# A twelve-stage transformer kernel: transposing x before it is normalised, centred weights, a second search among the additions, integer slot numbers

## What is computed

```python
# block 0: 7 experts of 512 slots each, the 8th kind passes the token on
x = x + 0.5 * _L0_ffn_ref(_layernorm(x), router_w, router_b, experts_inter, experts_out)
# block 3: 8 linear experts, each token goes to its best two, unweighted
logits = x @ gate_w.T
probs = jax.nn.softmax(logits, axis=-1)
_, topk_idx = jax.lax.top_k(probs, 2)
...
h = _grouped_matmul(moe_in, w_up, seg_ids)
moe_out = _grouped_matmul(h, w_down, seg_ids)
```

## Time and profile before

| | us |
|---|---|
| median of 3 runs (2966.19 to 2968.7) | 2966.94 |
| the profiled execution, its own time | 2966.22 |
| its span in the profile | 2964.5 |
| PE busy, 79% of the span | 2356.5 |
| DVE busy, 68% | 2009.4 |
| ACT busy, 63% | 1861.4 |
| POOL busy, 33% | 974.5 |

### The profile page before, as it was taken

One profiled execution on the slowest core, in us unless ns is written; L12 is line 12 of the kernel. 1 busy time (PEld: TensorE's weight loads), 2 busy tenths in 40 slices (PEclk: granted clock), 3 DMA queues, 4 the chain that ended last, 5 costly groups with the idle time before them and its releaser, 6 DMA issues. The chain is left out here.

```text
span 2964.5 us, 44016 instructions
## 1 busy us (share of the span) xinstructions
PE 2356.5 (79%) x13097; PEld 1220.5 (41%) x13097; DVE 2009.4 (68%) x5780; ACT 1861.4 (63%) x4759; POOL 974.5 (33%) x1296
## 2 busy tenths in 40 slices
PE   4647484738888878499999999997858888888887
PEld 4425453512222246244444444444524444444452
DVE  4616633759899947566666666665568999998854
ACT  2124223327777763377777777776539999999964
POOL 2553275344353332400000000003644444444436
PEclk8778596559999985799999999999769999999979
DMA  6330232023223200000000000000011111111001
GB/s 173 78 53 1 89 69 39 0 42 75 53 49 77 51 8 1 30 1 1 1 1 1 1 1 1 1 1 1 1 34 30 29 30 30 29 30 30 1 1 29
DMA packets 230444, 86.76 MB, mean 29 GB/s; under 512 B 175362, under 2 KB 223298, under 8 KB 230210
## 3 DMA queue, kind: packets, MB, share of 16 engines
q1 hardware_dynamic: 215104, 74.74, 10.8%
q0 software_dynamic: 9856, 7.58, 1.8%
q10 hardware_dynamic: 5250, 1.62, 0.3%
HBM read 26.47 MB, written 15.50 MB: 14 GB/s over the span
## 5 line engine op out<-in xcount | busy, mean ns | idle before, releaser
L2375 ACT ACTIVATE s_pT<-s_ps_t 128x512 f32<-128x512 f32 x1024 | 625.1, 638 | 139.7 <-PE s_ps_t L1975 123.9
L2128 DVE TENSOR_REDUCE s_neg_max<-s_ps_a 128x1 f32<-128x512 f32 x1024 | 666.1, 682 | 63.0 <-PE s_ps_a L1941 53.0
L2366 ACT ACTIVATE s_first<-s_ps_a,s_neg_max 128x512 f32<-128x512 f32 x512 | 390.5, 763 | 25.1 <-DVE s_neg_max L2128 23.4
L2784 ACT ACTIVATE s_e<-s_e,s_neg_max 128x128 f32<-128x128 f32 (+3 forms) x512 | 283.2, 555 | 165.6 <-DVE s_neg_max L2684 163.3
L1987 PE MATMUL s_ps_t<-ident,s_first 128*128 128x128 f32 x2048 | 316.1, 285 | 83.8 <-ACT s_pT L2375 71.3
L2297 POOL TENSOR_SCALAR s_first<-s_first,s_rec 128x512 f32<-128x512 f32 x128 | 232.3, 1815 | 365.6 <-DVE s_rec L2134 359.6
L2684 DVE CUSTOM_DVE_ANT_0 s_e<-s_ps_a,w_alibi 128x128 f32<-128x128 f32 (+3 forms) x512 | 230.7, 487 | 110.9 <-PE s_ps_a L2554 109.9
L1941 PE MATMUL s_ps_a<-s_lanesT 64*128 64x512 bf16 x1024 | 275.2, 401 | 37.3 <-DMA s_lanesT<-n_lanes 20.4
L1987 PEld LDWEIGHTS s_ps_t<-ident,s_first 128*128 128x128 f32 x2048 | 220.8, 141 | 183.5 <-ACT s_pT L2375 141.5
L2002 PE MATMUL s_ps_o<-s_pT,n_v_pad 128*32 128x512 f32 x2048 | 275.9, 612 | 12.2 <-ACT s_oT L2381 12.2
L139 POOL TENSOR_TENSOR s_rstd<-s_ve,minus_half 128x4 f32<-128x4 f32 x24 | 26.4, 1099 | 678.8 <-DVE s_ve L126 678.2
(11 more groups left out here) (382 smaller groups left out, 4079.7 us busy)
## 6 DMA issues: line engine op xcount, KB each, us to landing
s_token_rows<-s_rows SPq DMA_DIRECT2D x4, 1088.0 KB, 5.4
s_x_rows<-x SPq DMA_DIRECT2D x4, 1024.0 KB
x<-s_x_rows SPq DMA_DIRECT2D x8, 512.0 KB, 6.1
s_Wi<-L_ffn_experts_inter SPq DMA_DIRECT2D x2, 1792.0 KB, 8.0
x<-L_attn_x SPq DMA_DIRECT2D x4, 512.0 KB, 7.9
out<-x SPq DMA_DIRECT2D x4, 512.0 KB, 5.3
s_lanesT<-n_lanes SPq DMA_TRANSPOSE x64, 4.1
s_shiftedT<-n_lanes SPq DMA_TRANSPOSE x64, 2.4
```

Source lines behind the costliest of these rows:

```text
L2128: dve.tensor_reduce(neg_max[:, column(n):column(n) + 1], sa[n % NA][:], AX.X, ALU.max, negate=True).then_inc(s.max_ready, 1)
L2366: act.activation(first[:, g % NF, n % PU, :], sa[n % NA][:], ACT.Exp, bias=neg_max[:, n:n + 1], accum_out=sum1[:, n % (NR * PU):n % (NR * ...
L2375: act.activation(pT[:, n % NP, :], st[n % NK][:], ACT.Exp).then_inc(s.probs_ready, 1)
L2784: act.activation(part, part, ACT.Exp, bias=neg_max[:, n:n + 1], scale=-1.0, accum_out=total[:, n:n + 1]).then_inc(s.first_ready, 1)
```

## The change

Five things are changed.

- In the capacity and linear stages TensorE transposes x itself. Subtracting the mean is moved into the weights: `setup` makes a matrix `center` (identity minus 1/128) and multiplies the router's, the gate's and the linear experts' weights by it. The reciprocal deviation is multiplied onto the logits on VectorE, and in the linear stage onto the mask too. The linear stage has no `xn` and no normalisation any more, and two PSUM buffers for the turned batch (one is `y4`). The capacity stage still normalises, for the rows that are gathered, but behind the copies.
- The linear stage's search for the second half of the tokens is cut in four pieces that stand among the additions.
- The numbering of slots uses int32, a shift and a bit mask; `code` is laid out tile by tile.
- ScalarE's exponentials are moved in both stages.
- Semaphores are handed out from a list of free ones, the lowest first, instead of by name. (`lasting` is added, and nothing calls it.)

```diff
@@ -62,18 +62,33 @@
...
-    for n in names.split():
-        if n not in ALL_SEMS.made:
-            ALL_SEMS.made[n] = ALL_SEMS.ctx.enter_context(nc.semaphore(n))
-    return namedtuple("Semaphores", names)(*[ALL_SEMS.made[n] for n in names.split()])
-def clear(nc, s):
-    cleared = range(min(h.num for h in s), max(h.num for h in s) + 1)
...
-    nc.all_engine_barrier(sems_to_clear=cleared)
+    names = names.split()
+    while len(ALL_SEMS.free) < len(names):
+        ALL_SEMS.made += 1
+        ALL_SEMS.free.append(ALL_SEMS.ctx.enter_context(nc.semaphore(f"stage{ALL_SEMS.made}")))
+    taken, ALL_SEMS.free = ALL_SEMS.free[:len(names)], ALL_SEMS.free[len(names):]
+    return namedtuple("Semaphores", names)(*taken)
...
+def clear(nc, s, last=False):
+    numbers = [h.num for h in s]
...
+    nc.all_engine_barrier(sems_to_clear=range(min(numbers), max(numbers) + 1))
+    ALL_SEMS.free = sorted([*s, *ALL_SEMS.free], key=lambda h: h.num)
...
@@ -210,22 +227,36 @@
...
+                pool.tensor_scalar(center[:], G.ident[:], -1.0 / D, None, ALU.add).then_inc(s.made, 1)
...
-                pe.wait_ge(s.made, 1)
+                pe.wait_ge(s.made, 3)
...
+                pe.matmul(psC[:, 0:KINDS], center[:], raw_router[:], start=True, stop=True).then_inc(s.router_psum, 1)
                 multiply_linear(pe)
...
+                pe.matmul(psC[:, 0:KINDS], center[:], raw_gate[:], start=True, stop=True).then_inc(s.gate_psum, 1)
                 turn_adapters(pe)
+                center_linear(pe, center)
...
+                dve.tensor_copy(G.routerT[:], psC[:, 0:KINDS]).then_inc(s.router_copied, 1)
...
+                halve_linear(dve)
...
+                dve.tensor_copy(G.gateT[:], psC[:, 0:KINDS]).then_inc(s.gate_copied, 1)
+                copy_adapters(dve)
                 copy_linear(dve)
-                copy_adapters(dve)
...
@@ -451,12 +491,23 @@
...
-    def copy(dve):
+    def halve(dve):
...
-            dve.tensor_scalar(G.M[:, 4 * i:4 * i + 4, :], ps[i][:], 0.5, None, ALU.mult).then_inc(s.m_copied, 1)
...
+            dve.tensor_scalar(M[:, 4 * i:4 * i + 4, :], ps[i][:], 0.5, None, ALU.mult).then_inc(s.m_halved, 1)
+    def center_rows(pe, center):
+        for i in range(2):
+            pe.wait_ge(s.m_halved, i + 1)
+            pe.matmul(ps[i][:], center[:], M[:, 4 * i:4 * i + 4, :], start=True, stop=True).then_inc(s.centered_psum, 1)
+    def copy(dve):
+        for i in range(2):
+            dve.wait_ge(s.centered_psum, i + 1)
+            dve.tensor_copy(G.M[:, 4 * i:4 * i + 4, :], ps[i][:]).then_inc(s.m_copied, 1)
...
@@ -469,12 +520,14 @@
...
         logits_ps, turned_ps = [pb(f"l{h}", [P, 512]) for h in range(HALVES)], pb("xT", [P, L])
...
-        minus, xn, xnT = sb("minus", [P, NT]), sb("xn2", [P, 2, TB, D]), sb("xnT2", [D, B, L])
+        xT = sb("xT", [D, B, L])
+        turned = [turned_ps[:], y[NY - 1][:].rearrange("p e d -> p (e d)")]
...
@@ -485,16 +538,30 @@
...
-                def choose(h):
+                def shift_logits(h):
                     at, wide = half(h), [P, WT, E]
...
-                    do(dve.tensor_copy(logits[:, at], logits_ps[h][:, 0:WT * E].rearrange("p (t e) -> p t e", e=E)))
+                    dve.wait_ge(s.rstd_ready, HB * (h + 1))
+                    do(dve.tensor_tensor(logits[:, at], logits_ps[h][:, 0:WT * E].rearrange("p (t e) -> p t e", e=E),
+                                         N.rstd[:, at].unsqueeze(2).to_broadcast(wide), ALU.mult))
                     softmax_rows(do, dve, s.shifted, probs[:, at], logits[:, at], m[:, at], WT)
+                def divide(h):
+                    at, wide = half(h), [P, WT, E]
...
-                    top2_mask(do, dve, T, probs[:, at], mask[:, at], WT)
+                def first_expert(h):
+                    find_first(do, dve, T, probs[:, half(h)], mask[:, half(h)], WT)
+                def second_expert(h):
+                    at, wide = half(h), [P, WT, E]
+                    find_second(do, dve, T, probs[:, at], mask[:, at], WT)
+                    do(dve.tensor_tensor(mask[:, at], mask[:, at], N.rstd[:, at].unsqueeze(2).to_broadcast(wide), ALU.mult))
...
@@ -502,6 +569,8 @@
...
+                        dve.wait_ge(s.xT_psum, t // TB + 1)
...
@@ -516,14 +585,24 @@
                 for b in range(B):
                     N.tile_statistics(dve, do, G.x, b)
                     N.aggregate(dve, do, b)
-                dve.wait_ge(s.xn_ready, NT)
-                for h in range(HALVES):
-                    choose(h)
+                shift_logits(0)
+                divide(0)
+                first_expert(0)
+                second_expert(0)
                 for t in range(0, NT, 2):
                     for e in range(E // 2):
                         add_expert(t, e)
                         add_expert(t + 1, e)
+                    if t == 0:
+                        shift_logits(1)
+                    if t == 4:
+                        divide(1)
+                    if t == 6:
+                        first_expert(1)
+                    if t == 8:
+                        second_expert(1)
             @block.gpsimd
             def _(pool):
                 do = Chain(pool, s.p_chain)
@@ -532,10 +611,6 @@
...
-                    pool.wait_ge(s.rstd_ready, b + 1)
-                    do(pool.tensor_tensor(minus[:, at], N.mv[:, at, 0], N.rstd[:, at], ALU.mult))
-                    do(pool.tensor_scalar(minus[:, at], minus[:, at], -1.0, None, ALU.mult))
-                    pool.engine_nop().then_inc(s.minus_ready, 1)
...
@@ -553,18 +628,9 @@
...
+                def copy_xT(b):
...
+                    act.activation(xT[:, b, :], turned[b % 2], ACT.Copy).then_inc(s.xT_ready, 1)
...
@@ -579,31 +645,28 @@
...
-                normalise(0)
...
-                    if b + 1 < B:
-                        normalise(b + 1)
-                    copy_xnT(b)
-                for h in range(HALVES):
-                    exp(h)
+                    copy_xT(b)
+                exp(0)
...
+                    if t == 3:
+                        exp(1)
...
-                    pe.wait_ge(s.xn_ready, TB * (b + 1))
-                    if b:
-                        pe.wait_ge(s.xnT_ready, b)
-                    for t in range(TB):
-                        last = pe.transpose(turned_ps[:, t * P:(t + 1) * P], xn[:, b % 2, t, :], G.ident[:])
...
+                    if b >= 2:
+                        pe.wait_ge(s.xT_ready, b - 1)
+                    for t in range(TB):
+                        last = pe.transpose(turned[b % 2][:, t * P:(t + 1) * P], G.x[:, b * TB + t, :], G.ident[:])
+                    last.then_inc(s.xT_psum, 1)
...
-                    pe.wait_ge(s.xnT_ready, b + 1)
+                    pe.wait_ge(s.xT_ready, b + 1)
...
@@ -740,11 +805,10 @@
...
-                    pe.wait_ge(s.xn_ready, TB * (b + 1))
...
-                        last = pe.transpose(turned_ps[b % 2][:, t * P:(t + 1) * P], xn[:, b * TB + t, :], G.ident[:])
+                        last = pe.transpose(turned_ps[b % 2][:, t * P:(t + 1) * P], G.x[:, b * TB + t, :], G.ident[:])
...
@@ -824,14 +888,18 @@
...
+                    dve.wait_ge(s.rstd_ready, HB * (h + 1))
...
-                                         G.router_b[:].unsqueeze(1).to_broadcast(wide), ALU.add))
+                                         N.rstd[:, at].unsqueeze(2).to_broadcast(wide), ALU.mult))
+                    do(dve.tensor_tensor(logits[:, at], logits[:, at], G.router_b[:].unsqueeze(1).to_broadcast(wide), ALU.add))
                     softmax_rows(do, dve, s.shifted, probs[:, at], logits[:, at], m[:, at], WT)
...
-                    top2_mask(do, dve, T, probs[:, at], mask[:, at], WT)
+                    find_first(do, dve, T, probs[:, at], mask[:, at], WT)
+                    find_second(do, dve, T, probs[:, at], mask[:, at], WT)
...
@@ -855,23 +923,16 @@
...
-                    do(dve.tensor_tensor(incl[:], te(prefix), incl[:], ALU.add))
-                    do.free(dve.scalar_tensor_tensor(out=kept[:], in0=incl[:], scalar=float(CAP), in1=mask[:],
+                    do(dve.scalar_tensor_tensor(out=number_i[:], in0=te(prefix), scalar=-1.0, in1=incl[:],
+                                                op0=ALU.add, op1=ALU.add))
+                    do.free(dve.scalar_tensor_tensor(out=kept[:], in0=number_i[:], scalar=float(CAP - 1), in1=mask[:],
...
-                    def steps(to, width, n):
-                        do(dve.tensor_scalar(to, incl[:], float(width), None, ALU.is_gt))
-                        for i in range(2, n):
-                            do(dve.scalar_tensor_tensor(out=to, in0=incl[:], scalar=float(width * i), in1=to,
-                                                        op0=ALU.is_gt, op1=ALU.add))
-                        do(dve.scalar_tensor_tensor(out=incl[:], in0=to, scalar=float(-width), in1=incl[:],
-                                                    op0=ALU.mult, op1=ALU.add))
```

(21 more changed lines are left out.)

71 lines of the change are left out of this document (42 added, 29 removed).

## The result

The kernel with the change took 2936.33 us, the median of 4 runs (2931.7 to 2940.54), against 2966.57 of the kernel before: 1.04% faster, ratio 0.9896 with an interval of 0.9876 to 0.9917. That is 30.2 us against 29.9 in the prediction's sum. Some of this closeness is luck: the profiled run gained 25.7, and single executions of this kernel differ by more than the error of the sum. The four times lie in two pairs, 2932 and 2940; the profiled run (2940.54, span 2938.8) is of the upper one; and the same kernel measured again gave 2940.96 against 2967.22.

The account below looks back on a forecast made before the run. Routing was taken as paced by TensorE at 1.2 GHz, with numbering alone on the capacity path; setup +2.0, barriers -4.3, capacity stages -10.6 and linear stages -17.0 sum to -29.9, giving 2936.3 us, range 2922 to 2946.

Parts of the forecast that it names:

- the prediction's sum: Whole kernel: +2.0 - 4.3 - 10.6 - 17.0 = -29.9 us, for a time of 2936.3 us.
- Barriers: 16 barriers: semaphores cleared fall from 1186 to 381 in all, at 5.4 ns each, -4.3 us.
- Setup: End of setup: two added 128x512 matmuls and a copy behind the last product lengthen the path, +2.0 us.
- Capacity stages: Both capacity stages: VectorE resumes earlier (gain 1.2 each) and numbering is shorter (4.05 each), -10.6 us for both.
- Rival (b): Capacity stages: integer numbering saves nothing and scattered reads slow the marks, 4.4 us lost per stage, 2945 us; chance 0.08.
- Linear stages, routing: Linear stages' start: first addition at 2094.8 instead of 2107.69, the first three pairs end earlier, gain 12.7 us per stage.
- rival (a): Routing in capacity and linear stages: TensorE's clock stays high, at 2.4 GHz, 2924 us; chance 0.10.
- Linear stages, the search between additions: Linear stages' additions: each inserted search costs its length less VectorE's 1.56 us wait, 4.2 us per stage.
- rival (d): Linear stages' additions: the long search idles TensorE, its clock stays at 1.2 GHz, up to 3005 us; chance 0.03.
- the mean 0.34 over six: Second search: 0.34 us of stretching beside POOL for each of six instructions reading two SBUF tensors, length 4.64 us.
- Rival (c): Linear stages: inserted searches hold POOL up too, leaving only routing's 6.4 us of 8.5, 2941 us; chance 0.06.
- The pairs' pitch: Linear stages' additions: each pair of tiles keeps 3.72 us, 2.16 of VectorE work and 1.56 waiting for TensorE.

Follow-up runs that it names:

- all three improvements: One wait for the turned x, the second search in three parts and earlier exponentials, together on the changed kernel: 2920.05 us, ratio 0.9831.

## Why the prediction was right, point by point

**Barriers**, -4.3: measured 6.94 - 2.57 = -4.4, and the kernel that clears 130 each time shows that this time is paid in full.

**Setup**, +2.0: +1.8 by its own rows; +0.5 in the stage.

**Capacity stages**, -10.6: first gathers 5.3 and 5.4 us earlier, as the step says (1.2 and 4.05), the stages 10.7 shorter together. Rival (b), the integers, is refuted in both its halves: shift and mask took 0.28 and 0.29 us, and the mark that now reads `code` scattered takes 1.22 us, as it did before.

**Linear stages, routing**: first addition 22.4 us into the stage, forecast 22.7; the third pair ended 2097.10 - 2062.70 = 34.4 us in, forecast 34.2. The clock over the first 20 us was 0.54 and 0.51, so rival (a) is refuted as it was put: TensorE was 97% busy, and the clock fell even so. The Trainium skill, TensorE: Matmul & The Clock Gate, section "Part 4: PE-mode transpose", says that a transpose doesn't count as busy in the way that other work does. The runs agree: in the kernels with all three improvements the same stretch ran at 0.54 without and at 1.00 with one wide product per batch. The stretch also holds products of 8 columns; no run tells their part from the transposes'.

**Linear stages, the search between additions**, the step that failed. The prediction has a cost of 1.1 for the first search and 3.1 for the second, 4.2 in all. The total was near, 3.9 and 4.6 us, but made otherwise: the searches were shorter than priced, and a fall of the clock that had no price made up for it. By the pairs' ends the first search cost 0.3. The second cost 3.6 and 3.9, of which 2.3 remain when the clock doesn't fall (13.6 us for three pairs against 3 x 3.79); in the second stage the division, forecast as free, cost 0.35. The rule itself, an insertion less VectorE's wait, held: 2.02 - 1.63 = 0.4 and 3.98 - 1.63 = 2.35, and TensorE stood still for 0.39 and 2.36 us. What the step had wrong is the searches' length, and that it put the clock at nothing: rival (d) named the fall and gave it 0.03 as a lasting one; it came, and lasted 3.4 us. The stretching beside POOL came, but weaker: 0.79, 0.50, 0.70 and 0.50 us for four instructions of the second search, 0.28 and 0.29 for the two others; the search took 3.9 us, not 4.64; the mean 0.34 over six is 0.22 here ((0.50 + 0.21 + 0.41 + 0.21) / 6).

By the Trainium skill, SBUF — State Buffer, section "SBUF: two separate sides", the engine that starts first has the pair of ports for its whole instruction, and the other one waits. The trace agrees with this in all six. POOL beside the second search:

```profile
2104.87 0.62 POOL L621 TENSOR_TENSOR x<-x,s_z 128x128 f32<-128x128 f32 x1 [0.49 <-DVE x L577]
2105.46 0.72 POOL L618 TENSOR_TENSOR s_z<-s_z 128x256 f32<-128x256 f32 x1
2106.26 0.46 POOL L619 TENSOR_TENSOR s_z<-s_z 128x128 f32<-128x128 f32 x1
2106.79 0.45 POOL L621 TENSOR_TENSOR x<-x,s_z 128x128 f32<-128x128 f32 x1
2107.21 0.88 POOL L618 TENSOR_TENSOR s_z<-s_z 128x256 f32<-128x256 f32 x1
2108.17 0.46 POOL L619 TENSOR_TENSOR s_z<-s_z 128x128 f32<-128x128 f32 x1
```

Each of the four stretched instructions began while one of POOL's was running and ended 0.14 or 0.15 us behind its end (2105.54 + 0.79 against 2105.46 + 0.72, and so on). The two that kept their length, at 2104.90 and 2107.22, began within 0.03 us of one of POOL's, and there POOL's was the longer one: 0.62 and 0.88 us, where the same lines take 0.45 and 0.72 on the median. So an instruction was not stretched by a mean, as the step has it, but by what was left of POOL's.

**Rival (c)**, that the insertions eat up the gain of the early start, is refuted by the run with both searches ahead of the additions: its stages are 1.8 us or more longer.

**The pairs' pitch**, 3.72, was taken over unchanged and was 3.79. The diff shows the reason, and I had not priced it: a wait that is always met, on VectorE's path between TensorE's product and the addition. 32 pairs x 0.07 = 2.2 us, most of the 2.9 by which the linear stages fell short (-14.1 without their clears, against -17.0).

**The sum.** In the profiled run -25.7: the linear stages 2.9 short, untouched stages 2.8 longer (segment attention +2.1), setup 1.5 better, against -29.9. The median of the runs, -30.2, was nearer, presumably because two of the four fell on lower levels of other stages or had no clock fall; the profiles are of the upper ones, so this is argued, not shown. The range, 2922 to 2946, held both.
